# The scan stage of a two-layer kernel: a weight quantised in a turned layout, with its scale rows loaded back from memory

## The chip, the cores and the metric

The kernel runs on one core of a Trainium2 chip. The metric is the device time of one execution in microseconds (us). Before the change the median of three runs is 2079.48 us (2079.25 to 2079.97).

## The reference, cut to what matters

Two layers act on x of shape (2, 4096, 512). In the first, a state-space branch and a quantised linear branch read the same normalised x:

```
x1 = xn @ w1.T + b1;  z = silu(conv(x1));  v = silu(xn @ v1.T + bv1)
h  = h * sigmoid(A) + z_t * B;  y = sum(h * C) + D * z_t      # a scan over 4096 tokens, 512 channels, 16 states
x  = x + (y * v) @ w2.T + b2 + quant(xn) @ quant(Wf).T + bf
```

`quant` takes each row in blocks of 32 elements: scale = max(max|block| / 7.5, 1e-30), the block divided by its scale is rounded to the nearest value of a 6-bit grid, and multiplied by the scale again. For the weight Wf (512 x 512, rows are output features) this gives 16 scales a row. The second layer (linear attention and a gated feed-forward) is not touched.

## The kernel before, in words

The program has four phases, one after the other on each engine's queue: project (x to z and v), scan (z to y), mix (the rest of layer one and the keys of layer two), and the second layer. The change lies in `phase_scan` (L664 to L931).

The scan goes over 64 octets of 8 channels. For octet o, TensorE issues three products of 128x512, each seen as two passes in the trace: `own(o + 1)` (L901, z times the into-table, to the bank that the recurrence reads), the product with the Toeplitz table (L919) and the product of the states with the out-table (L922), which ends y of the octet (semaphore `y_full`). Beside them:

- SyncE loads z (256 KB an octet, L717) six octets ahead, when `y_full` of octet o - 6 is there.
- GpSimd makes the three tables of an octet (L755), three octets ahead at most. TensorE's `own` waits for all three.
- VectorE runs the recurrence (`scan(o + 1)`, L773, two instructions), and behind it in each octet one extra step of the weight's preparation.
- ScalarE takes y out of its bank (`take(o)`, L843) and issues its store to memory (L847). There are four y tiles (`Y = 4`), and `take` of octet o waits until the store of octet o - 4 has landed. TensorE's Toeplitz product of octet o waits for the take of octet o - 2 (`y_done`). ScalarE's queue also issues the weight loads, one 256 KB piece at a time.

The places are octet numbers written out by hand:

```
def take(o):
    act.wait_ge(y_full, o + 1)
    if o >= Y:
        act.wait_ge(y_stored[o % Y], 16 * (o // Y))
```

The feed-forward weight goes this way: ScalarE loads it in its natural layout (output features on partitions) to `wf_nat` at octets 1 to 4 (L860). VectorE quantises it in nine steps at octets 10 to 18 (L792 to L809): a reduce to the block maxima, two steps on 64 scales, a product with the inverse scales, four rounding steps on the 128x2048 tile, a product with the scales. TensorE turns it by 16 transposes at octets 24 to 27 (L908, four banks). ScalarE rounds each bank to the high part (L876), and VectorE subtracts for the low part (L824). At octets 32 to 39 the same split is made for two other weights (ScalarE L852, VectorE L778).

GpSimd has one piece of other work near: at its octet 20, `clear_sums` (three memsets, L1109 and L1111).

Of the kernel before, what the change touches and what calls it, by code (L numbers as in the profile page):

```python
# [3 lines left out]
P = 128  # L4
# [659 lines left out]
def phase_scan(nc, sh, ins, scr, keep, banks, areas, late, mix):  # L664
# [5 lines left out]
    def sem(name):  # L670
        return nc.alloc_semaphore(name)
# [6 lines left out]
    zo += [first_weight.tile(f"c_z{i}", [P, NCH]) for i in range(3, Z)]  # L678
    yo = [first_weight.tile(f"c_y{i}", [P, NCH]) for i in range(Y)]
    q_max = first_weight.tile("c_q_max", [P, KT * D // QBLOCK])  # L680
    q_scale = first_weight.tile("c_q_scale", [P, KT * D // QBLOCK])
    q_inv = first_weight.tile("c_q_inv", [P, KT * D // QBLOCK])
    wf_nat = turned_x.tile("c_wf_nat", [P, KT * D])
    q_work = turned_x.tile("c_q_work", [P, KT * D])
    w2, wf, wk, wv = late["w2"], late["wf"], late["wk"], late["wv"]
    w2_raw, wk_raw = late["w2_raw"], late["wk_raw"]

    z_in = [sem(f"c_z_in{i}") for i in range(Z)]
    y_stored = [sem(f"c_y_stored{i}") for i in range(Y)]
# [5 lines left out]
    wf_in = sem("c_wf_in")  # L695
    w_hi, w_lo = keep["w_hi"], keep["w_lo"]
    HI = 2 * KT
    q_step, f_turned, f_hi = sem("c_q_step"), sem("c_f_turned"), sem("c_f_hi")

    FB, YB, SB = banks[0:4], banks[4:6], banks[6:8]  # L700
    into_t, toep_t, out_pow, mask8 = keep["into_t"], keep["toep_t"], keep["out_pow"], keep["mask8"]
    ident = keep["ident"]
    z_of = scr["z"].rearrange("(o c) r n -> o (c r) n", c=OCTET)
    y_of = scr["y"].rearrange("(o c) m n -> o (c m) n", c=OCTET)
    TURN_AT, WEIGHTS_AT, QUANTISE_AT = 24, 32, 10
    QUANTISED_AT, WEIGHT_PIECES_AT, BIASES_AT = 1, 6, 30
    MIX_IN_AT, MIX_PREPARE_AT, MIX_BANKS_AT, MIX_HEAD_AT = 38, 40, 42, 61
    MIX_TURN_AT = {56: 0, 60: 1}
# [57 lines left out]
    def vector(dve):  # L766
        def scan(o):
            dve.wait_ge(own_full, o + 1)
            if o >= 2:
                dve.wait_ge(y_full, o - 1)  # L770
            rate = keep["decay"][:, o:o + 1].broadcast_to([P, NCB - 1])
            for b in range(B):
                nc.vector.tensor_tensor_scan(state[o % 2][:, b, 1:], rate, SB[o % 2][:, b * NCB:(b + 1) * NCB - 1],  # L773
                                             0.0, ALU.mult, ALU.add).then_inc(state_done, 1)

        def weight_low(i, kt, tile, raw):
            dve.wait_ge(w_hi, HI + KT * i + kt + 1)
            nc.vector.tensor_tensor(tile[:, 1, kt, :], raw[:, kt, :], tile[:, 0, kt, :].bitcast(F32),  # L778
                                    ALU.subtract).then_inc(w_lo, 1)

        blocks = wf_nat[:, :].rearrange("p (b e) -> p b e", e=QBLOCK)
        NB = KT * D // QBLOCK

        def wide(tile):
            return tile[:, :].unsqueeze(2).broadcast_to([P, NB, QBLOCK])

        def quantise_step(k):
            dve.wait_ge(wf_in, 16 * KT)
            if k:
                dve.wait_ge(q_step, k)  # L790
            if k == 0:
                ins_ = nc.vector.tensor_reduce(q_max[:, :], blocks, AX.X, ALU.max, apply_absolute_value=True)  # L792
            elif k == 1:
                ins_ = nc.vector.tensor_scalar(q_scale[:, :], q_max[:, :], 1.0 / FP6_MAX, SCALE_EPS, ALU.mult, ALU.max)
            elif k == 2:
                ins_ = nc.vector.reciprocal(q_inv[:, :], q_scale[:, :])
            elif k == 3:
                ins_ = nc.vector.tensor_tensor(blocks, blocks, wide(q_inv), ALU.mult)
            elif k == 4:
                ins_ = nc.vector.tensor_scalar(q_work[:, :].bitcast(U32), wf_nat[:, :].bitcast(U32), EXPONENT_BITS,  # L800
                                               None, ALU.bitwise_and)
            elif k == 5:
                ins_ = nc.vector.tensor_scalar(q_work[:, :], q_work[:, :], 1.0, ROUND_MAGIC, ALU.max, ALU.mult)
            elif k == 6:
                ins_ = nc.vector.tensor_tensor(wf_nat[:, :], wf_nat[:, :], q_work[:, :], ALU.add)
            elif k == 7:
                ins_ = nc.vector.tensor_tensor(wf_nat[:, :], wf_nat[:, :], q_work[:, :], ALU.subtract)
            else:
                ins_ = nc.vector.tensor_tensor(blocks, blocks, wide(q_scale), ALU.mult)  # L809
            ins_.then_inc(q_step, 1)  # L810

        for i in range(2):
            nc.vector.memset(state[i][:, :, 0:1], 0.0).then_inc(zeroed, 1)
        dve.wait_ge(zeroed, 2)
        scan(0)
        for o in range(NO):
            if o + 1 < NO:
                scan(o + 1)
            if QUANTISE_AT <= o < QUANTISE_AT + 9:
                quantise_step(o - QUANTISE_AT)  # L820
            if TURN_AT <= o - 2 < TURN_AT + KT:
                kt = o - 2 - TURN_AT
                dve.wait_ge(f_hi, kt + 1)
                nc.vector.tensor_tensor(wf[:, 1, kt, :], FB[kt][:, :], wf[:, 0, kt, :].bitcast(F32), ALU.subtract)\  # L824
                  .then_inc(w_lo, 1)
            if WEIGHTS_AT <= o < WEIGHTS_AT + 2 * KT:
                i, kt = divmod(o - WEIGHTS_AT, KT)
                weight_low(i, kt, *((w2, w2_raw), (wk, wk_raw))[i])
            if o == MIX_IN_AT:
                mix["shift"]()  # L830
            if MIX_PREPARE_AT <= o < MIX_PREPARE_AT + 3 * mix["steps"]:
                mix["prepare_step"](*divmod(o - MIX_PREPARE_AT, mix["steps"]))
            if o - 2 in MIX_TURN_AT:
                mix["low_q"](MIX_TURN_AT[o - 2])
            if o == MIX_HEAD_AT:
                mix["gate_front"](0)

    def scalar(act):
# [17 lines left out]
        for o in range(NO):  # L856
            take(o)
            if QUANTISED_AT <= o < QUANTISED_AT + KT:
                t = o - QUANTISED_AT
                act.dma_start(wf_nat[:, t * D:(t + 1) * D], ins["L0_ffn_weight"][t * P:(t + 1) * P, :])\  # L860
                   .then_inc(wf_in, 16)
            if o == WEIGHT_PIECES_AT:
                for h in range(2):
                    act.wait_ge(*project["z"][h])
                    act.wait_ge(*project["v"][h])
                act.wait_ge(*project["powers"])
            if WEIGHT_PIECES_AT <= o < WEIGHT_PIECES_AT + 2 * 3 * KT and (o - WEIGHT_PIECES_AT) % 2 == 0:
                i, kt = divmod((o - WEIGHT_PIECES_AT) // 2, KT)
                tile, name, done = pieces[i]
                act.dma_start(tile[:, kt, :], ins[name][:, kt, :]).then_inc(done, 16)  # L870
            if o in (BIASES_AT, BIASES_AT + 2, BIASES_AT + 4):
                mix["load_bias"]((o - BIASES_AT) // 2)
            if TURN_AT <= o - 1 < TURN_AT + KT:
                kt = o - 1 - TURN_AT
                act.wait_ge(f_turned, kt + 1)
                nc.scalar.activation(wf[:, 0, kt, :], FB[kt][:, :], ACT.Copy).then_inc(f_hi, 1)  # L876
            if WEIGHTS_AT <= o < WEIGHTS_AT + 2 * KT:
                i, kt = divmod(o - WEIGHTS_AT, KT)
                weight_high(i, kt, *((w2, w2_raw), (wk, wk_raw))[i])
# [12 lines left out]
            if o >= NO - 2:  # L892
                mix["set_sums"](o - NO + 3)

    def tensor(pe):
# [5 lines left out]
            pe.matmul(SB[o % 2][:, :], into[o % TABS][:, :, :].rearrange("p c s -> p (c s)"), zo[o % Z][:, :],  # L901
                      start=True, stop=True).then_inc(own_full, 1)

        def turn_weight(kt):
            if kt == 0:
                pe.wait_ge(q_step, 9)
            for ot in range(KT):
                mm = pe.transpose(FB[kt][:, ot * P:(ot + 1) * P], wf_nat[:, ot * D + kt * P:ot * D + (kt + 1) * P],  # L908
                                  ident[:, :])
            mm.then_inc(f_turned, 1)  # L910

        own(0)
        pe.wait_ge(*project["v_taken"])
        for o in range(NO):
            if o + 1 < NO:
                own(o + 1)
            if o >= 2:
# [3 lines left out]
            pe.wait_ge(state_done, B * (o + 1))  # L921
            pe.matmul(YB[o % 2][:, :], outof[o % TABS][:, :, :].rearrange("p c m -> p (c m)"),  # L922
                      state[o % 2][:, :, :].rearrange("p b n -> p (b n)"), start=False, stop=True).then_inc(y_full, 1)
            if TURN_AT <= o < TURN_AT + KT:
                turn_weight(o - TURN_AT)
            if o == MIX_BANKS_AT:
                mix["open_banks"]()
            if o in MIX_TURN_AT:
# [1225 lines left out]
def two_layer_kernel(nc, ins, out):  # L2154
# [3 lines left out]
    def dram(name, shape, dt=F32):  # L2158
# [3 lines left out]
        "x": ins["L0_attn_x"],  # L2162
        "out": out,
        "rows": dram("scr_rows", [sh.NG, 2, sh.GT, P]),
        "kern": dram("scr_kern", [NO, OCTET, 2 * CHUNK]),
        "z": dram("scr_z", [D, CHUNK, sh.NCH]),
        "v": dram("scr_v", [D, CHUNK, sh.NCH]),
# [109 lines left out]
```

## Time and profile before

| | |
|---|---|
| median of three runs | 2079.48 us |
| the profiled execution's own time | 2080.59 us |
| its span, first to last instruction | 2078.8 us |
| TensorE busy | 2063.7 us (99%) |
| VectorE busy | 1523.1 us (73%) |
| ScalarE busy | 1095.0 us (53%) |
| GpSimd busy | 840.9 us (40%) |
| moved by DMA | 263.47 MB |

The profile is of one execution. Times are from the start of the span. DVE is VectorE, ACT ScalarE, POOL GpSimd, PE TensorE's products, PEld its weight loads, SPq and ACTq the DMA issues of SyncE and ScalarE. The scan phase lies between about 369 and 540 us. Time between a DMA's issue and its data's arrival is called landing.

### The profile page before, as it was taken

What the parts mean: (1) busy time and instruction counts of PE and PEld (TensorE: products, weight loads), DVE (VectorE), ACT (ScalarE), POOL (GpSimd) and SP (SyncE); (2) the same over time, 40 slices, a digit from 0 to 9 for tenths busy, and PEclk for the clock granted to TensorE, in tenths of its full rate; (3) what the DMA queues carried; (4) which work ended last, traced back from release to release, by engine and by line L of the source; (5) the groups of instructions that cost most, each with busy time, mean ns of one, the idle gap of its engine ahead of it and who ended that gap; (6) DMA issues with size and microseconds to landing.
All of it is one profiled execution on the core that took longest, in us unless ns stands there. A gap on an engine that the chain in (4) does not pass through costs nothing.

```text
span 2078.8 us, 27463 instructions
## 1 busy us (share of the span) xinstructions
PE 2063.7 (99%) x9263; PEld 1645.9 (79%) x9263; DVE 1523.1 (73%) x2973; ACT 1095.0 (53%) x1842; POOL 840.9 (40%) x842
## 2 busy tenths in 40 slices
PE   9999999999999999999999999999999999999998
PEld 7887888444688888888888888788888888888887
DVE  6998775666787777776777875677777676677776
ACT  4555556223455555555555555755555555555553
POOL 1011110455545454554444453144444444444444
PEclk9999999999999999999999999999999999999999
DMA  5666662976533333333333332422222222222211
GB/s 199 251 220 226 202 210 103 292 254 208 176 122 102 108 116 103 131 102 102 122 119 105 115 119 101 152 71 72 71 72 74 90 91 86 88 71 72 71 41 41
DMA packets 179750, 263.47 MB, mean 127 GB/s; under 512 B 20377, under 2 KB 110745, under 8 KB 177050
## 3 DMA queue, kind: packets, MB, share of 16 engines
q1 hardware_dynamic: 166488, 238.18, 34.7%
q10 hardware_dynamic: 13122, 23.53, 3.1%
q8 instruction: 74, 1.21, 0.3%
q14 instruction: 66, 0.54, 0.1%
HBM read 160.88 MB, written 100.79 MB: 126 GB/s over the span
## 4 chain that ended last, share of the span: by engine, by line
PE 89%; DVE 5%; ACT 2%; issue 2%; POOL 1%; DMA 1%; SPq 0%; POOLq 0%; ACTq 0%
PE bank L102 23%; PE bank L104 23%; PE bank L103 23%; PE bank L1512 7%; PE bank L2068 3%; PE bank L901 3%; PE bank L922 3%; PE bank L919 3%; PE bank L1468 2%; PE bank L645 1%; DVE e_w_lo L1895 0%; DVE d_x L1364 0%; DVE d_xq L1335 0%; DVE d_stats L1366 0%; PE bank L1526 0%
## 5 line engine op out<-in xcount | busy, mean ns | idle before, releaser
L102 PE MATMUL bank<-e_ring,e_w_hi 128*128 128x512 f32 x512 | 200.8, 392 | 0.0
L103 PE MATMUL bank<-e_ring,e_w_hi 128*128 128x512 f32 x512 | 199.3, 389 | 0.0
L104 PE MATMUL bank<-e_ring,e_w_lo 128*128 128x512 f32 x512 | 199.3, 389 | 0.0
L1512 PE MATMUL bank<-d_kh,d_nat 128*128 128x512 f32 x768 | 191.1, 398 | 0.0
L1788 POOL TENSOR_TENSOR e_x<-e_x,e_beta 128x512 f32<-128x512 f32 x64 | 91.5, 1449 | 220.7 <-ACT e_y L1831 220.7
L1133 POOL TENSOR_TENSOR rstd<-d_var_eps,neg_half 128x1 f32<-128x1 f32 x64 | 35.7, 558 | 340.7 <-DVE d_var_eps L1375 340.7
L1842 ACT ACTIVATE e_kr<-bank 128x512 f32<-128x512 f32 x64 | 38.0, 594 | 247.6 <-PE bank L104 247.6
L1512 PEld LDWEIGHTS bank<-d_kh,d_nat 128*128 128x128 f32 x768 | 139.7, 188 | 26.9
L1913 DVE TENSOR_TENSOR e_ring<-e_mixed,e_ring 128x512 fp32r<-128x512 f32 x128 | 93.5, 731 | 88.0 <-ACT e_ring L1806 87.9
L1770 POOL TENSOR_TENSOR e_x<-e_x,e_ff 128x512 f32<-128x512 f32 x64 | 83.4, 1304 | 174.9 <-DVE e_ff L1979 174.9
L1380 DVE TENSOR_TENSOR d_nat<-d_xn,d_nat 128x512 fp32r<-128x512 f32 x64 | 86.0, 1345 | 78.1 <-ACT d_nat L1240 78.1
L1904 DVE SCALAR_TENSOR_TENSOR e_mixed<-e_xt,cols,e_prev 128x512 f32<-128x512 f32 x128 | 104.0, 813 | 41.3 <-ACT e_prev L1817 40.8
L1222 ACT ACTIVATE d_xt<-bank 128x512 f32<-128x512 f32 x64 | 38.3, 598 | 166.7 <-PE bank L1468 166.6
L773 DVE TENSOR_TENSOR_SCAN c_state<-decay,bank 128x255 f32<-128x255 f32 x128 | 80.4, 670 | 53.2 <-PE bank L901 53.1
L311 POOL TENSOR_TENSOR b_rstd<-b_var_eps,neg_half 128x4 f32<-128x4 f32 x16 | 16.2, 1011 | 247.2 <-DVE b_var_eps L367 247.2
L102 PEld LDWEIGHTS bank<-e_ring,e_w_hi 128*128 128x128 f32 x512 | 96.1, 188 | 20.4 <-issue 0.9
L1806 ACT ACTIVATE e_ring<-e_mixed 128x512 fp32r<-128x512 f32 x128 | 80.8, 632 | 59.7 <-DVE e_mixed L1904 57.4
L1774 POOL TENSOR_TENSOR e_y<-e_y,e_att 128x512 f32<-128x512 f32 x64 | 107.1, 1673 | 12.7 <-DVE e_att L1998 12.7
L104 PEld LDWEIGHTS bank<-e_ring,e_w_lo 128*128 128x128 f32 x512 | 96.1, 188 | 20.1
L103 PEld LDWEIGHTS bank<-e_ring,e_w_hi 128*128 128x128 f32 x512 | 96.1, 188 | 19.3
L102 PE MATMUL bank<-e_w_hi,e_keys 128*128 128x512 f32 x256 | 103.7, 405 | 0.2 <-DVE e_ff L1979 0.2
L102 PE MATMUL bank<-d_w,d_ut 128*128 128x512 f32 x256 | 100.2, 391 | 2.1 <-POOL d_ut L1121 2.1
(226 smaller groups left out, 6300.0 us busy)
## 6 DMA issues: line engine op xcount, KB each, us to landing
scr_v<-b_vt SPq DMA_DIRECT2D x64, 256.0 KB, 2.7
scr_z<-b_zt SPq DMA_DIRECT2D x64, 256.0 KB, 2.1
c_z<-scr_z SPq DMA_DIRECT2D x64, 256.0 KB, 4.3
scr_y<-c_y ACTq DMA_DIRECT2D x64, 256.0 KB, 4.0
d_x<-in_L_attn_x SPq DMA_DIRECT2D x64, 256.0 KB, 3.6
d_v<-scr_v SPq DMA_DIRECT2D x32, 512.0 KB, 5.2
scr_x<-d_x SPq DMA_DIRECT2D x64, 256.0 KB, 2.3
scr_xnt<-d_xt SPq DMA_DIRECT2D x32, 512.0 KB, 4.1
```

The costliest lines, as they stand in the source:

```text
L102: eng.matmul(out, lhs[hi], rhs[hi], start=first, stop=False, skip_group_check=onto)
L103: eng.matmul(out, lhs[hi], rhs[lo], start=False, stop=False, skip_group_check=onto)
L104: return eng.matmul(out, lhs[lo], rhs[hi], start=False, stop=last, skip_group_check=onto)
L773: nc.vector.tensor_tensor_scan(state[o % 2][:, b, 1:], rate, SB[o % 2][:, b * NCB:(b + 1) * NCB - 1], 0.0, ALU.mult, ALU.add).then_inc(sta ...
L1380: nc.vector.tensor_tensor(nat[q][:, 1, :], xn[N % 2][:, :], nat[q][:, 0, :].bitcast(F32), ALU.subtract).then_inc(nat_lo, 1)
L1512: mm = pe.matmul(BG[c][:, :], s[:, i, cols], r[:, j, :], start=M % NTB == 0 and i == j, stop=M % NTB == NTB - 1 and i == 1, skip_group_che ...
L1770: nc.gpsimd.tensor_tensor(x2[h][:, t, :], x2[h][:, t, :], ff[t % 2][:, :], ALU.add).then_inc(base_done, 1)
L1774: nc.gpsimd.tensor_tensor(y[t][:, :], y[t][:, :], att[t % 2][:, :], ALU.add).then_inc(sum_done, 1)
L1788: nc.gpsimd.tensor_tensor(x2[h][:, t, :], x2[h][:, t, :], beta[:, :], ALU.add).then_inc(shifted, 1)
L1806: nc.scalar.activation(ring[slot][:, 0, kt, :], src, ACT.Copy).then_inc(hi_done, 1)
L1904: nc.vector.scalar_tensor_tensor(mixed[kt % 2][:, :], current(g % 2, kt), mu[:, kt:kt + 1], prev[kt % 2][:, :], ALU.mult, ALU.add).then_in ...
L1913: nc.vector.tensor_tensor(ring[slot][:, 1, kt, :], src, ring[slot][:, 0, kt, :].bitcast(F32), ALU.subtract).then_inc(lo_done, 1)
```

## The change

The weight also comes from the host in the turned layout (`ffn_turned`, input features on partitions), and the quantisation works on that layout in `wf_raw`, which is the place of the low part of `wf`. The block maxima are still found on the natural layout, at octet 6. Scales and inverse scales are computed at octets 7 and 8 into 32 columns for each of the four groups of 128 rows, and turned by four VectorE transposes of 32x32 blocks at octet 9. At octet 10 ScalarE's queue stores them in four DMAs to a 32x512 array in memory. At octet 13 it loads from there two tiles of 128x2048 (the inverse scales to `q_work`, the scales to `wf_nat`), 1 MB each: partition group s of 32 reads the same row of 2048 numbers. Six VectorE steps at octets 24 to 29 then quantise the turned weight. The 16 transposes on TensorE go. The turned weight's four pieces of 256 KB are loaded at octets 7, 9, 11 and 13 on ScalarE's queue. The high parts are rounded at octets 30 to 33 and the low parts at 31 to 34.

```
@@ phase_scan: tiles, semaphores, banks, octets @@
-    q_scale = first_weight.tile("c_q_scale", [P, KT * D // QBLOCK])
-    q_inv = first_weight.tile("c_q_inv", [P, KT * D // QBLOCK])
+    q_cols = first_weight.tile("c_q_cols", [P, KT, QBLOCK])
+    q_turned = first_weight.tile("c_q_turned", [P, KT, QBLOCK])
...
-    q_step, f_turned, f_hi = sem("c_q_step"), sem("c_f_turned"), sem("c_f_hi")
-    FB, YB, SB = banks[0:4], banks[4:6], banks[6:8]
+    q_step, f_hi = sem("c_q_step"), sem("c_f_hi")
+    wf_raw_in = sem("c_wf_raw_in")
+    YB, SB = banks[4:6], banks[6:8]
...
-    TURN_AT, WEIGHTS_AT, QUANTISE_AT = 24, 32, 10
+    ROUNDED_AT, WEIGHTS_AT, SCALES_AT, SCALES_OUT_AT, ROWS_IN_AT, QUANTISE_AT = 29, 32, 6, 10, 13, 24
+    SCALE_STEPS, QUANTISE_STEPS = 3 + KT, 6
@@ VectorE @@
+        def scale_step(k):
+            if k:
+                dve.wait_ge(q_step, min(k, 3))
+            scales = q_cols[:, :, KT * KT:2 * KT * KT]
+            if k == 0:
+                dve.wait_ge(wf_in, 16 * KT)
+                ins_ = nc.vector.tensor_reduce(q_max[:, :], wf_nat[:, :].rearrange("p (b e) -> p b e", e=QBLOCK), AX.X,
+                                               ALU.max, apply_absolute_value=True)
+            elif k == 1:
+                for t in range(KT):
+                    ins_ = nc.vector.tensor_scalar(scales[:, t, :].rearrange("p (s k) -> p k s", k=KT),
+                                                   q_max[:, t * KT * KT:(t + 1) * KT * KT]
+                                                   .rearrange("p (k s) -> p k s", k=KT),
+                                                   1.0 / FP6_MAX, SCALE_EPS, ALU.mult, ALU.max)
+            elif k == 2:
+                ins_ = nc.vector.reciprocal(q_cols[:, :, 0:KT * KT], scales)
+            else:
+                ins_ = nc.vector.transpose(q_turned[:, k - 3, :], q_cols[:, k - 3, :])
+            ins_.then_inc(q_step, 1)
+
         def quantise_step(k):
-            dve.wait_ge(wf_in, 16 * KT)
-            if k:
-                dve.wait_ge(q_step, k)
+            dve.wait_ge(q_step, SCALE_STEPS + k)
+            wf_turned = wf_raw[:, :, :].rearrange("p k d -> p (k d)")
             if k == 0:
-                ins_ = nc.vector.tensor_reduce(q_max[:, :], blocks, AX.X, ALU.max, apply_absolute_value=True)
...
-            elif k == 3:
-                ins_ = nc.vector.tensor_tensor(blocks, blocks, wide(q_inv), ALU.mult)
+                dve.wait_ge(wf_in, 16 * (2 * KT + 2))
+                dve.wait_ge(wf_raw_in, 16 * KT)
+                ins_ = nc.vector.tensor_tensor(wf_turned, wf_turned, q_work[:, :], ALU.mult)
...
             else:
-                ins_ = nc.vector.tensor_tensor(blocks, blocks, wide(q_scale), ALU.mult)
+                ins_ = nc.vector.tensor_tensor(wf_turned, wf_turned, wf_nat[:, :], ALU.mult)
@@ VectorE, the loop over octets @@
-            if QUANTISE_AT <= o < QUANTISE_AT + 9:
+            if SCALES_AT <= o < SCALES_AT + 3:
+                scale_step(o - SCALES_AT)
+            if o == SCALES_AT + 3:
+                for k in range(3, SCALE_STEPS):
+                    scale_step(k)
+            if QUANTISE_AT <= o < QUANTISE_AT + QUANTISE_STEPS:
                 quantise_step(o - QUANTISE_AT)
-            if TURN_AT <= o - 2 < TURN_AT + KT:
-                kt = o - 2 - TURN_AT
+            if ROUNDED_AT <= o - 2 < ROUNDED_AT + KT:
+                kt = o - 2 - ROUNDED_AT
                 dve.wait_ge(f_hi, kt + 1)
-                nc.vector.tensor_tensor(wf[:, 1, kt, :], FB[kt][:, :], wf[:, 0, kt, :].bitcast(F32), ALU.subtract)\
+                nc.vector.tensor_tensor(wf[:, 1, kt, :], wf_raw[:, kt, :], wf[:, 0, kt, :].bitcast(F32), ALU.subtract)\
@@ ScalarE, the loop over octets @@
+            if o == SCALES_OUT_AT:
+                act.wait_ge(q_step, SCALE_STEPS)
+                for s in range(P // QBLOCK):
+                    act.dma_start(scr["f_scales"].rearrange("c (t s i) -> s c t i", t=KT, s=P // QBLOCK)[s],
+                                  q_turned[s * QBLOCK:(s + 1) * QBLOCK, :, :]).then_inc(wf_in, 16)
+            if o == ROWS_IN_AT:
+                act.wait_ge(wf_in, 16 * 2 * KT)
+                for w, tile in enumerate((q_work, wf_nat)):
+                    rows = bass.AP(scr["f_scales"].tensor, w * KT * KT * D,
+                                   [[KT * D, P // QBLOCK], [0, QBLOCK], [1, KT * D]])
+                    act.dma_start(tile[:, :], rows).then_inc(wf_in, 16)
...
+            if WEIGHT_PIECES_AT <= o < WEIGHT_PIECES_AT + 2 * KT and (o - WEIGHT_PIECES_AT) % 2:
+                kt = (o - WEIGHT_PIECES_AT) // 2
+                act.dma_start(wf_raw[:, kt, :], ins["ffn_turned"][:, kt, :]).then_inc(wf_raw_in, 16)
...
-            if TURN_AT <= o - 1 < TURN_AT + KT:
-                kt = o - 1 - TURN_AT
-                act.wait_ge(f_turned, kt + 1)
-                nc.scalar.activation(wf[:, 0, kt, :], FB[kt][:, :], ACT.Copy).then_inc(f_hi, 1)
+            if ROUNDED_AT <= o - 1 < ROUNDED_AT + KT:
+                kt = o - 1 - ROUNDED_AT
+                act.wait_ge(q_step, SCALE_STEPS + QUANTISE_STEPS)
+                nc.scalar.activation(wf[:, 0, kt, :], wf_raw[:, kt, :], ACT.Copy).then_inc(f_hi, 1)
@@ TensorE @@
-        def turn_weight(kt):
-            if kt == 0:
-                pe.wait_ge(q_step, 9)
-            for ot in range(KT):
-                mm = pe.transpose(FB[kt][:, ot * P:(ot + 1) * P], wf_nat[:, ot * D + kt * P:ot * D + (kt + 1) * P],
-                                  ident[:, :])
-            mm.then_inc(f_turned, 1)
...
-            if TURN_AT <= o < TURN_AT + KT:
-                turn_weight(o - TURN_AT)
@@ two_layer_kernel, kernel @@
+        "f_scales": dram("scr_f_scales", [QBLOCK, D]),
...
+    laid["ffn_turned"] = raw["L0_ffn_weight"].T.reshape(KT, P, 512).transpose(1, 0, 2)
```

## Rows read from the trace of the kernel before

**Rows 1.** The page: busy time by engine, and the chain that ended last by line.
```profile
PE 2063.7 (99%) x9263; PEld 1645.9 (79%) x9263; DVE 1523.1 (73%) x2973; ACT 1095.0 (53%) x1842; POOL 840.9 (40%) x842
PE bank L102 23%; PE bank L104 23%; PE bank L103 23%; PE bank L1512 7%; PE bank L2068 3%; PE bank L901 3%; PE bank L922 3%; PE bank L919 3%; PE bank L1468 2%; PE bank L645 1%; DVE e_w_lo L1895 0%; DVE d_x L1364 0%; DVE d_xq L1335 0%; DVE d_stats L1366 0%; PE bank L1526 0%
```

**Rows 2.** The chain of waits in the scan: start us, us, what.
```profile
378.36 0.86 PE bank L901 x2
...
406.68 0.86 PE bank L901 x2
...
427.42 0.86 PE bank L901 x2
...
435.15 0.86 PE bank L901 x2
...
447.20 0.86 PE bank L901 x2
```

**Rows 3.** Timeline, 406 to 425 us: start, us, engine, line, op [idle before].
```profile
406.18 2.27 DVE L798 TENSOR_TENSOR c_wf_nat<-c_wf_nat,c_q_inv 128x2048 f32<-128x2048 f32 x1
406.77 1.95 POOL L755 TENSOR_TENSOR c_into<-into_t,consts 128x128 f32<-128x128 f32 x1 [1.45 <-PE bank L922]
...
409.03 0.40 POOL L755 TENSOR_TENSOR c_outof<-out_pow,consts 128x128 f32<-128x128 f32 x1
...
409.53 1.10 PE L901 MATMUL bank<-c_z,c_into 128*128 128x512 f32 x2 [0.28 <-issue]
...
420.78 0.98 POOL L1111 MEMSET d_kacc<- 128x512 f32 x2
...
421.27 2.26 DVE L809 TENSOR_TENSOR c_wf_nat<-c_wf_nat,c_q_scale 128x2048 f32<-128x2048 f32 x1
...
421.72 2.07 POOL L755 TENSOR_TENSOR c_into<-into_t,consts 128x128 f32<-128x128 f32 x1
...
424.61 1.10 PE L901 MATMUL bank<-c_z,c_into 128*128 128x512 f32 x2 [0.90 <-issue]
```

**Rows 4.** Timeline of two undisturbed ScalarE takes and of one scan.
```profile
373.25 0.60 ACT L843 ACTIVATE c_y<-bank 128x512 f32<-128x512 f32 x1 [4.04 <-PE bank L922]
...
389.56 1.26 DVE L773 TENSOR_TENSOR_SCAN c_state<-decay,bank 128x255 f32<-128x255 f32 x2 [1.31 <-PE bank L901]
...
406.72 0.60 ACT L843 ACTIVATE c_y<-bank 128x512 f32<-128x512 f32 x1 [1.98 <-PE bank L922]
```

**Rows 5.** Timeline: weight piece, reduce and small steps; then octet 32.
```profile
383.55 0.35 ACTq L860 DMA_DIRECT2D c_wf_nat<-in_L_ffn_weight  x1
...
398.46 2.26 DVE L792 TENSOR_REDUCE c_q_max<-c_wf_nat 128x64 f32<-128x2048 f32 x1
...
399.04 0.40 POOL L755 TENSOR_TENSOR c_into<-into_t,consts 128x128 f32<-128x128 f32 x1 [1.45 <-PE bank L922]
...
401.80 0.27 DVE L794 TENSOR_SCALAR c_q_scale<-c_q_max 128x64 f32<-128x64 f32 x1
...
460.61 0.62 ACT L852 ACTIVATE d_w<-d_w_raw 128x512 fp32r<-128x512 f32 x1
...
461.27 0.69 DVE L778 TENSOR_TENSOR d_w<-d_w_raw,d_w 128x512 fp32r<-128x512 f32 x1 [1.60 <-ACT d_w L852]
```

**Rows 6.** DMA issues of the whole run: names, queue, count, KB, us to landing.
```profile
c_z<-scr_z SPq DMA_DIRECT2D x64, 256.0 KB, 4.3
scr_y<-c_y ACTq DMA_DIRECT2D x64, 256.0 KB, 4.0
b_xc<-in_x_turned SPq DMA_DIRECT2D x14, 1024.0 KB, 7.1
b_rows<-scr_rows SPq DMA_DIRECT2D x14, 512.0 KB, 5.4
```

**Rows 7.** Windows: stretch, busy by engine (count), clock, DMA share, GB/s.
```profile
16.00:18.00 2.00, 2.00 (x11) 1.62 (x10) 2.00 (x4) 2.00 (x5) 0.00 (x0) 1.00 1.06 427
...
370.00:380.00 10.00, 10.00 (x25) 4.37 (x24) 5.67 (x10) 1.79 (x3) 4.29 (x10) 1.00 1.05 358
```

More of the change, by code:

```diff
@@ L685, in phase_scan @@
     w2, wf, wk, wv = late["w2"], late["wf"], late["wk"], late["wv"]
-    w2_raw, wk_raw = late["w2_raw"], late["wk_raw"]
+    w2_raw, wf_raw, wk_raw = late["w2_raw"], late["wf_raw"], late["wk_raw"]
     z_in = [sem(f"c_z_in{i}") for i in range(Z)]
@@ L697, in phase_scan @@
     HI = 2 * KT
-    q_step, f_turned, f_hi = sem("c_q_step"), sem("c_f_turned"), sem("c_f_hi")
-    FB, YB, SB = banks[0:4], banks[4:6], banks[6:8]
+    q_step, f_hi = sem("c_q_step"), sem("c_f_hi")
+    wf_raw_in = sem("c_wf_raw_in")
+    YB, SB = banks[4:6], banks[6:8]
     into_t, toep_t, out_pow, mask8 = keep["into_t"], keep["toep_t"], keep["out_pow"], keep["mask8"]
-    ident = keep["ident"]
     z_of = scr["z"].rearrange("(o c) r n -> o (c r) n", c=OCTET)
     y_of = scr["y"].rearrange("(o c) m n -> o (c m) n", c=OCTET)
-    TURN_AT, WEIGHTS_AT, QUANTISE_AT = 24, 32, 10
+    ROUNDED_AT, WEIGHTS_AT, SCALES_AT, SCALES_OUT_AT, ROWS_IN_AT, QUANTISE_AT = 29, 32, 6, 10, 13, 24
+    SCALE_STEPS, QUANTISE_STEPS = 3 + KT, 6
     QUANTISED_AT, WEIGHT_PIECES_AT, BIASES_AT = 1, 6, 30
@@ L779, in weight_low @@
                                     ALU.subtract).then_inc(w_lo, 1)
[L781 to L785, printed above, removed]
+        def scale_step(k):
[17 more added lines that the diff above has]
+            ins_.then_inc(q_step, 1)
@@ L793, in quantise_step @@
             elif k == 1:
-                ins_ = nc.vector.tensor_scalar(q_scale[:, :], q_max[:, :], 1.0 / FP6_MAX, SCALE_EPS, ALU.mult, ALU.max)
+                ins_ = nc.vector.tensor_scalar(q_work[:, :].bitcast(U32), wf_turned.bitcast(U32), EXPONENT_BITS,
+                                               None, ALU.bitwise_and)
             elif k == 2:
-                ins_ = nc.vector.reciprocal(q_inv[:, :], q_scale[:, :])
+                ins_ = nc.vector.tensor_scalar(q_work[:, :], q_work[:, :], 1.0, ROUND_MAGIC, ALU.max, ALU.mult)
@@ L797, in quantise_step @@
             elif k == 3:
-                ins_ = nc.vector.tensor_tensor(blocks, blocks, wide(q_inv), ALU.mult)
+                ins_ = nc.vector.tensor_tensor(wf_turned, wf_turned, q_work[:, :], ALU.add)
             elif k == 4:
[L800 to L807, printed above, removed]
+                ins_ = nc.vector.tensor_tensor(wf_turned, wf_turned, q_work[:, :], ALU.subtract)
```

## The prediction

> **What bounds the kernel now.** I read the page first. TensorE is busy for 2063.7 us of 2078.8 and the chain that ended last runs over its products almost alone [rows 1], so an edit counts by what it takes from TensorE's queue or makes that queue wait. Next the chain in the scan. An undisturbed octet is 2.575 us: its first product starts at 378.36 and, 11 octets on, at 406.68 [rows 2]. Six passes of 0.43 us fill that time, so there TensorE is the bound. The chain shows two disturbed stretches. From 406.68 to 427.42 seven octets take 20.74 us where 18.02 are due: 2.72 us lost. From 435.15 to 447.20 four octets take 12.05 for 10.30: 1.75 us, the 16 transposes [rows 2].
>
> The timeline explains the first stretch. A two-input VectorE step on the 128x2048 tile runs from 406.18 to 408.45. GpSimd's table product beside it takes 1.95 us, and ends 0.27 us after that step [rows 3]; beside the reduce at 398.46 the same table product takes 0.40 [rows 5]. The tables of that octet are complete at 409.43, and TensorE, 0.28 us idle, starts at 409.53 [rows 3]. So the loss is GpSimd held up by the rounding steps, not the recurrence being late. The worst gap, 0.90 us at 424.61, has one more cause: the memsets of `clear_sums` (0.98 us from 420.78) pushed the table product into the last step, which began at 421.27 [rows 3].
>
> **What goes.** The 16 transposes: -1.75 us, all on TensorE's queue, with nothing in their place.
>
> **What moves.** Six large VectorE steps of the same kinds and sizes (2.27 and 2.26 us for those shown in [rows 3], the other four likewise the same operations on the same shape) go from octets 13 to 18 to octets 24 to 29. GpSimd makes tables there too, so their 2.72 us come again, less the part of the memsets, which stay at octet 20 in an idle stretch of GpSimd. Without them the first table of that octet would be done before 421.27, and one table product of 0.40 us less would be queued behind the step: -0.4 us (bounds: 0 and -1.0, all of the memset). Both inputs of the two products with the scales are now full tiles; before, one was read as a broadcast. 2.27 and 2.26 us for those against about the same for the others leaves nothing to price.
>
> **What VectorE does new at octets 6 to 9.** The reduce (2.26 us [rows 5]) needs the fourth weight piece, issued at 383.55; transfers of that size on this queue land in 4.0 us at the median [rows 6]; taking 5.3 to be careful gives 388.9. It then ends at 391.1, and the recurrence due at 389.56 [rows 4] starts 1.5 us late. TensorE needs its result four product pairs later: own at 388.5, needed at 388.5 + 2.575 + 2 x 0.86 = 392.8, and the recurrence takes 1.26 [rows 4], so it may start up to about 391.4. Hidden, with 0.3 to spare (bounds 0 and +0.3). Four scale steps on 16 columns and the inverse: 0.27 us for 64 columns [rows 5] gives at most 1.1 and 0.5, hidden in the 1.31 us that VectorE idles each octet [rows 4]. The four VectorE transposes are not in the trace; from below a 64-column step each (0.27), from above a 512-column subtract each (0.69 [rows 5]), so 1.1 to 2.8 us together; I take 1.1, hidden, at the other end about +0.1.
>
> **Octets 31 to 34.** The low parts now share octets 32 to 34 with those of the next weight. Today the ScalarE rounding is done 461.23 and VectorE waits 1.60 us for it [rows 5]. A second rounding in front adds 0.62 us. The recurrence behind is then some 1.5 us late instead of 0.9, at the edge of what is free: +0.1 us (0 to +0.4).
>
> **What the queue gets.** This decides. The take of octet 0 is at 373.25 and that of octet 13 at 406.72 [rows 4]. There ScalarE issues, in this order, the two row loads (2 x 1,048,576 bytes), the last turned-weight piece and then the store of y of octet 13. Its own waits are covered: the four small stores were issued at octet 10, 7.7 us earlier, and loads and stores here land in 4 to 5. The take of octet 17, due 10.3 us later at 417.0, waits until that store has landed, and on each DMA engine the store's bytes come behind the rows' bytes of the same queue. Behind the take waits the Toeplitz product of octet 19, due at 407.54 + 5 x 2.575 = 420.4, and with it everything on TensorE.
>
> How long the row loads hold the queue depends on how many of the 16 DMA engines share them, and no row shows a load of this form: the nearest have 128 partitions' rows outermost on both sides, the 1 MB load of 8 KB rows (7.1 us) and the 512 KB load in which every partition reads the same row (5.4 us) [rows 6]. The new source pattern has 4 outermost (four groups, then 32 repeats, then 8 KB). So from below it is spread like the nearest rows, over 16 engines; from above over 4, one for each group. A transfer has to be cut along a dimension that both sides have, the outer one, and 4 is all that this source offers: I take 4. That departs from the nearest rows on purpose, since they lack just this.
>
> An engine's rate: 358 GB/s in a stretch where the engines are full and loads and stores mix, 427 where only loads run [rows 7], a sixteenth of each is 22.4 and 26.7 GB/s; I take 24.5. On each of the four engines lie 524,288 bytes of rows, 16,384 of the weight piece and 16,384 of the store, and beside them six z loads (SyncE gets to issue those for y of octets 13 to 18) of 16,384 each: 655,360 bytes, 26.7 us. From 407.2 with 1.0 us for the arrival (a 256 KB store lands in 4.0 though its bytes need 0.7; I allow less since the queue is already running) that is 434.9. The take ends at 435.6, and TensorE has waited 435.6 - 420.4 = 15.2 us (29.3 us at the slow rate give 17.8, 24.5 at the fast one 13.0). The stores of octets 14 to 16 lie directly behind, 0.7 to 1.4 us apart, against 2.6 us an octet: no further wait. Z was loaded ahead meanwhile. The rows have landed before octet 24.
>
> The clock: it is granted in full in every stretch read, and the longest gap in those of the scan is 0.90 us [rows 3, 7]. A gap of 15 us may let it fall to the lower level, 1.2 GHz. One octet at half speed costs 2.6 us; bounds 0 and 2.6, I take 1.3.
>
> The Trainium skill, "DMA: Bandwidth & Descriptors", in its section on why a DMA increments its semaphore by 16, says that a transfer is divided along the slowest dimension over the largest number of engines up to 16 that divides both sides' counts; its table of recommendations warns of just such a small outermost dimension. By that rule the row loads run on 4 engines and the sum is the one below; by the nearest rows, taken as they are, it is that of the first rival. No row of this trace tests it.
>
> **Sum.** -1.75 - 0.4 + 0.1 + 15.2 + 1.3 = +14.5 us. The profiled execution took 2080.59 us (span 2078.8), so 2095.1; the median of the runs shown lies 1.1 us below it, which gives 2094.0.
>
> **Rivals.**
> 1. *The row loads spread over all 16 engines (not slower).* An engine has 131,072 + 32,768 + three z loads of 16,384 = 212,992 bytes, 8.7 us; the store lands at 416.9, before the take asks at 417.0, and 2.8 us of TensorE's lead lie behind that. What is left is -1.75 - 0.4 + 0.1: 2077.4. For it: the two nearest rows. Against: their outer 128. The wait decides from about 11 engines down: the take may start until 419.8, so 11.6 us, 284 KB an engine, of which some 100 are other traffic. With 8 engines it is 14.7 us and a wait of 3 us, about 2080. Chance 0.21, with 0.03 for something between.
> 2. *Four engines, and slow ones.* One engine reads the same 8 KB 32 times, beside z loads of 2 KB pieces. At half the rate the 26.7 us become 53 and the wait 42: 2121. For it: nothing in the trace; against: the 512 KB load that repeats one row for all partitions lands in 5.4 us [rows 6]. Chance 0.06.
> 3. The forecast: 0.70. Its own range, by rate and clock: 2089 to 2100.
>
> **How the numbers follow.** Leaving out only the slow case and the far edges, the range goes from just under rival 1 to above the forecast's upper end: 2076.5 to 2102. A difference counts from 0.2%, 4.2 us, which is about what a measurement of this kernel can tell from no change. Rival 1 is 2.1 us faster, so within; the forecast and rival 2 are slower: slower 0.76, same 0.22, faster 0.02.
>
> **What would show it.** The landing of the two c_q_work and c_wf_nat loads from scr_f_scales: above 20 us for the forecast, under 10 for rival 1. The landing of the y store at 408: some 27 us. One TensorE gap of 13 to 18 us before L919 near 420, and ScalarE's c_y waiting for the store (DMA scr_y) instead of for TensorE. A DMA share near 0.4 to 0.5 in that gap, not 1.0. Near octets 24 to 29 gaps in front of L901 of about 2.3 us in all, with table products of about 2 us on GpSimd; no matmul on consts and c_wf_nat. It is wrong if the store of octet 13 lands within 11 us; the step at fault is then the count of engines.

## The result, and the profile after

| | before | after |
|---|---|---|
| median of four timed runs | 2079.36 us (2079.25 to 2079.97) | 2101.86 us (2099.13 to 2104.87) |
| profiled execution, own time | 2080.59 us | 2100.61 us |
| its span, granted clock | 2078.8 us, 0.999 | 2098.8 us, 0.995 |

The ratio is 1.0106, with the interval 1.0095 to 1.0118: slower by 22.5 us in the medians. Between the two profiled executions it is 20.0 us: the scan takes 21.5 us more (from the take of octet 0 to that of the last octet, 371.66 to 560.69 against 373.25 to 540.77), and it begins 1.6 us earlier, behind code that the change doesn't touch. The first rows are the page of after; they answer to [rows 1].

```profile
PE 2066.9 (98%) x9247; PEld 1645.6 (78%) x9247; DVE 1522.4 (73%) x2980; ACT 1094.8 (52%) x1842; POOL 840.4 (40%) x842
PE bank L102 22%; PE bank L104 22%; PE bank L103 22%; PE bank L1533 7%; PE bank L2089 3%; PE bank L942 2%; PE bank L932 2%; PE bank L945 2%; PE bank L1489 2%; DMA scr_y<-c_y 2%; DVE e_w_lo L1916 0%; DVE d_x L1385 0%; DVE d_xq L1356 0%; DVE d_stats L1387 0%; PE bank L1547 0%
```

A DMA is now among what the chain runs over: `DMA scr_y<-c_y`, 2% of the span. TensorE has 16 instructions fewer and 3.2 us more busy time; its mean granted clock is 0.995 for 0.999, so some of its products ran slower. The chain of waits in order of time (start us, us, what) shows where, and answers to [rows 2]; in this kernel L932 is the product into the state, L942 the Toeplitz product, L945 the one out of the state, L860 ScalarE's take.

```profile
403.53 0.86 PE bank L942 x2
...
405.29 0.60 ACT c_y L860
...
407.12 31.55 DMA scr_y<-c_y
...
438.75 0.61 ACT c_y L860
...
439.40 2.08 PE bank L942 x2
441.48 1.71 PE bank L945 x2
443.19 1.71 PE bank L932 x2
...
447.83 0.86 PE bank L942 x2
```

From 403.53 to 447.83 eight octets take 44.30 us where 8 x 2.575 = 20.60 are due: 23.7 lost. The store of y of octet 13, issued at 407.12, lands after 31.55 us; in the run before, such a store lands in 4.0 at the median [rows 6]. ScalarE's and TensorE's timelines of that stretch:

```profile
407.12 3.49 ACTq L864 DMA_DIRECT2D scr_y<-c_y  x1
410.71 0.60 ACT L860 ACTIVATE c_y<-bank 128x512 f32<-128x512 f32 x1 [4.82 <-PE bank L945]
410.72 3.29 ACTq L898 DMA_DIRECT2D d_wk_raw<-in_L_attn_Wk  x1
414.05 5.90 ACTq L864 DMA_DIRECT2D scr_y<-c_y  x1
420.06 0.60 ACT L860 ACTIVATE c_y<-bank 128x512 f32<-128x512 f32 x1 [8.75 <-issue]
...
438.75 0.60 ACT L860 ACTIVATE c_y<-bank 128x512 f32<-128x512 f32 x1 [15.47 <-DMA scr_y<-c_y]
```

```profile
420.70 2.07 PE L942 MATMUL bank<-c_z,c_toep 128*128 128x512 f32 x2 [6.51 <-ACT c_y L860]
422.57 1.92 PE L945 MATMUL bank<-c_state,c_outof 128*128 128x512 f32 x2
...
425.50 1.02 PE L942 MATMUL bank<-c_z,c_toep 128*128 128x512 f32 x2
...
439.40 2.08 PE L942 MATMUL bank<-c_z,c_toep 128*128 128x512 f32 x2 [11.16 <-ACT c_y L860]
```

There are two gaps. Before the second, ScalarE waits 15.47 us for the landing of the store: the gap of the forecast. Before the first it waits for no semaphore at all. It is still issuing: the three DMA instructions from 407.12 on last 3.49, 3.29 and 5.90 us, where such an issue mostly takes 0.33 to 0.36 elsewhere, and the take of octet 15 sits behind them. Read with the windows of the same stretch, which answer to [rows 7]:

```profile
412.00:416.00 4.00, 2.20 (x6) 0.65 (x4) 1.81 (x3) 0.00 (x0) 1.12 (x3) 1.00 0.71 225
416.00:420.00 4.00, 0.00 (x0) 0.00 (x0) 0.00 (x0) 0.00 (x0) 0.00 (x0) 0.77 0.32 108
420.00:424.00 4.00, 3.29 (x4) 1.51 (x5) 0.00 (x0) 1.19 (x2) 0.00 (x0) 0.50 0.52 203
...
432.00:436.00 4.00, 0.00 (x0) 0.00 (x0) 0.00 (x0) 0.00 (x0) 0.00 (x0) 0.50 0.25 102
```

The last three numbers of a row are the granted clock, the DMA share and GB/s. In the last row no engine has any work, and the DMA share is a quarter: 4 of 16 engines, at 102 / 4 = 25.5 GB/s each. The z loads that SyncE issues between 404 and 440 us, on its own queue, land after 6.1 to 11.9 us; before the change they take 2.9 to 5.4. They are late, but far less than the store. The granted clock falls to 0.50 within each gap, and the products behind it run at 1.2 GHz (2.07 us for what takes 1.02 at 425.50).

The steps that the forecast hid are hidden. The timeline of VectorE at octets 6 to 9 answers to [rows 5]:

```profile
387.42 2.29 DVE L789 TENSOR_REDUCE c_q_max<-c_wf_nat 128x64 f32<-128x2048 f32 x1 [0.61 <-DMA c_wf_nat<-in_L_ffn_weight]
...
390.79 0.49 DVE L793 TENSOR_SCALAR c_q_cols<-c_q_max 128x16 f32<-128x16 f32 x4
...
392.35 0.52 DVE L798 RECIPROCAL c_q_cols<-c_q_cols 128x64 f32<-128x64 f32 x1
...
394.44 0.47 DVE L800 STREAM_TRANSPOSE c_q_turned<-c_q_cols 128x32 f32<-128x32 f32 x4
```

The chain knows no gap there. In the quantise stretch (octets 24 to 29) it does:

```profile
454.69 0.86 PE bank L932 x2
...
459.84 0.27 issue
460.11 1.10 PE bank L932 x2
...
474.29 0.32 issue
474.61 1.10 PE bank L932 x2
...
477.42 0.86 PE bank L932 x2
```

Four such gaps (0.27, 0.28, 0.31, 0.32), each followed by a product pair of 1.10 for 0.86; eight octets take 22.73 for 20.60, so 2.13 us, against 2.72 before. From 477.42 to 502 the chain has no gap at all.

### The profile page after: what moved, and what is told of

The parts are those of the page before. It is cut to its first block, busy times and chain, and to the rows that moved or that the text cites. A ratio compares the mean times of both kernels' runs of the same rounds, so it can differ in the third digit from the quotient of the medians.

```text
span 2098.8 us, 27441 instructions
## 1 busy us (share of the span) xinstructions
PE 2066.9 (98%) x9247; PEld 1645.6 (78%) x9247; DVE 1522.4 (73%) x2980; ACT 1094.8 (52%) x1842; POOL 840.4 (40%) x842
## 4 chain that ended last, share of the span: by engine, by line
PE 87%; DVE 5%; DMA 2%; ACT 2%; issue 2%; POOL 1%; SPq 0%; ACTq 0%; POOLq 0%
PE bank L102 22%; PE bank L104 22%; PE bank L103 22%; PE bank L1533 7%; PE bank L2089 3%; PE bank L942 2%; PE bank L932 2%; PE bank L945 2%; PE bank L1489 2%; DMA scr_y<-c_y 2%; DVE e_w_lo L1916 0%; DVE d_x L1385 0%; DVE d_xq L1356 0%; DVE d_stats L1387 0%; PE bank L1547 0%
## 5 line engine op out<-in xcount | busy, mean ns | idle before, releaser
L860 ACT ACTIVATE c_y<-bank 128x512 f32<-128x512 f32 x64 | 38.2, 596 | 139.1 <-PE bank L945 108.9
```

## The experiments

All ran beside the kernel before, whose medians in these comparisons are 2079.75 to 2080.16 us. The theory under test: the source pattern `[[KT * D, 4], [0, 32], [1, KT * D]]` puts both loads on 4 of 16 DMA engines, and all that passes through these four is late. Rivals: the repeated reading of one row is slow, or the order in the queue alone does it.

**e1_split: sixteen engines by smaller loads.** The same bytes in the same octet and queue; each load is cut in four, of 32 partitions, whose outer dimension is now the partition.

```
-                    rows = bass.AP(..., w * KT * KT * D, [[KT * D, P // QBLOCK], [0, QBLOCK], [1, KT * D]])
-                    act.dma_start(tile[:, :], rows).then_inc(wf_in, 16)
+                    for s in range(P // QBLOCK):
+                        rows = bass.AP(..., (w * KT + s) * KT * D, [[0, QBLOCK], [1, KT * D]])
+                        act.dma_start(tile[s * QBLOCK:(s + 1) * QBLOCK, :], rows).then_inc(wf_in, 16)
```

> The changed kernel with each 1 MB row load cut into four loads of 256 KB, one for each group of 32 partitions, at the same octet on the same queue: same bytes, same memory rows read 32 times, but the outermost count is 32 in place of 4. Theory (the row loads ran on 4 of the 16 DMA engines, and the y store of octet 13 queued behind them): TensorE's two waits near 414 and 428 us go, the DMA share near octet 13 is close to 1 for some 7 us in place of 0.25, the store lands in under 12 us, and what is left of the change is its gain: 2079.4 - 1.75 (transposes) - 0.6 (the quantise stretch as measured after) = 2077.0, within 2076 to 2079. Rival A (reading the same 8 KB row for 32 partitions is slow in itself) and rival B (2 MB more is too much for this stretch): about 2095 to 2105 as in the changed kernel.

2085.72 us (2084.62 to 2086.92, 7 runs), ratio 1.0029 [1.0017, 1.0040]. It is 16 us faster than after, and no window shows a quarter any more, so the number of engines is most of the cost. But 2077 is missed by 8.7. The chain holds one store of y:

```profile
410.93 14.56 DMA scr_y<-c_y
```

and the windows show why it needs 14.56 us:

```profile
412.00:416.00 4.00, 4.00 (x10) 1.82 (x10) 2.25 (x4) 1.26 (x3) 1.72 (x5) 1.00 1.01 229
416.00:420.00 4.00, 3.26 (x8) 1.14 (x6) 1.53 (x3) 0.00 (x0) 2.74 (x8) 1.00 1.02 241
...
424.00:428.00 4.00, 1.78 (x2) 0.84 (x3) 0.00 (x0) 1.06 (x2) 0.00 (x0) 0.50 1.05 405
```

All 16 engines are busy, and they move 229 to 241 GB/s; as soon as the rows are in, 405. So a second cost was uncovered: a load into 32 partitions occupies 16 engines at little over half their rate. TensorE waits 5.1 us for it and 0.7 for a z load, and the three product pairs behind take 2.5 us more than at the full clock: 8.3 of the 8.7. The Trainium skill, "SBUF — State Buffer", section "Door 1: The DMA port swizzle", says that partitions 0 to 31 (and 0 to 63) reach only 8 of the 16 ports on SBUF's DMA side, and measures 189 GB/s for 1 MiB into 32 partitions against 328 into 128. The trace agrees in size: 229 against 405, in mixed traffic. That the ports are the reason, no run here shows.

**f1_distinct and f2_allparts: reading or writing?** The first is e1 with 32 different source rows for each load (the scales are left out: it reads `x_turned`). The second is after's two 1 MB loads with the one row repeated for all 128 partitions, outermost (the same scales everywhere).

```
+                        rows = bass.AP(ins["x_turned"].tensor, (w * KT + s) * QBLOCK * KT * D, [[KT * D, QBLOCK], [1, KT * D]])
```

```
+                                   [[0, P], [1, KT * D]])
```

> The split form of the row loads (eight loads to 32 partitions each) with its source changed to 32 distinct 8 KB rows of the input for each load; the weight's scales are then not the right ones, all else is the same work. In the split form the DMA engines were busy (share 1.0) at only 209 to 250 GB/s from 410 to 422 us, and the y store of octet 13 took 14.6 us. Theory P (the writing side: 32 partitions at a time take no more than that): no change, store 13 to 16 us, GB/s 200 to 260 at share 1, 2085.5 (2083.5 to 2087.5). Theory R (the reading side: one memory row read by all engines at once is slow): GB/s rises to 350 or more, the store lands in under 11 us, and the time falls to 2077 to 2079.

> The changed kernel with each 1 MB load reading one and the same 8 KB row for all 128 partitions (outermost count 128), so two whole-tile loads and the wrong scales. Theory P (writing side): all partitions are reached at once, engines busy at 350 GB/s or more for some 7 us, y store of octet 13 in 8 to 11 us, 2077 to 2079. Theory R (reading side): the same row is read even more often, so 209 to 250 GB/s at share 1 again and 2084 or more. Both leave the four-engine theory alone: the share must not go to 0.25.

f1: 2085.66 us (2084.08 to 2086.74), ratio 1.0025, the same as e1, and its store of octet 13 lands after 15.09 us; where the rows are read plays no part. f2: 2078.09 us (2077.50 to 2078.83), ratio 0.9990 [0.9980, 1.0001]. Its windows, with one row read 128 times:

```profile
408.00:412.00 4.00, 4.00 (x11) 1.84 (x10) 2.05 (x4) 0.97 (x2) 2.07 (x6) 1.00 1.03 415
...
416.00:420.00 4.00, 3.21 (x8) 1.25 (x7) 2.33 (x4) 0.60 (x1) 2.74 (x8) 1.00 1.03 392
```

So 2 MB at that place and from one row are nearly free when they are spread over 16 engines and 128 partitions. Nearly: its store of octet 13 lands after 12.26 us (8 to 11 were expected) and TensorE waits 0.8. The first rival of the prediction described this kernel (2077.4), and it lay at the edge of its slack.

f2 differs from e1 in two things, 128 partitions for 32 and two loads for eight. The number of loads doesn't explain the rate: the transfers of 256 KB that follow the rows in e1, over 128 partitions each, run at 405 GB/s. It does add issuing time. Issuing eight row loads and the weight piece keeps ScalarE for 4.6 us before the store in e1, issuing two and the piece for 1.5 in f2; from the first row load's issue to the landing of the store it is 19.2 us in e1 and 13.8 in f2. How much of these 5.4 us is issuing isn't separated.

**e2_half: only one of the two loads split.** c_q_work stays in the narrow form, c_wf_nat is cut in four.

> The changed kernel with only the load of the scales cut into four, that of the inverse scales left in the form with 4 outermost. Theory: each of the four engines has 262,144 + 65,536 + 32,768 + five z loads of 16,384 = 442,368 bytes, at 25.5 GB/s 17.3 us; the store of octet 13 lands some 18 us after the row loads' issue, TensorE waits about 6 us once and loses 2 to 3 us to the clock: 2085.5 (2081 to 2090). The DMA share shows a stretch near 0.25 of under 10 us. Rivals A and B (same reads and bytes): 2095 to 2105.

2101.20 us (2101.18 to 2101.22), ratio 1.010: as slow as after. The expectation (2085.5) is missed. It counted half the narrow bytes as half the wait. The windows:

```profile
412.00:416.00 4.00, 4.00 (x11) 1.78 (x10) 2.52 (x4) 0.60 (x1) 1.51 (x5) 1.00 1.00 209
...
432.00:436.00 4.00, 0.00 (x0) 0.00 (x0) 0.00 (x0) 0.00 (x0) 0.00 (x0) 0.50 0.25 72
```

At first all 16 engines are busy at 209 GB/s; afterwards four of them are still at work alone, at 72 to 86 GB/s. The store of octet 13 lands after 30.83 us, and the issue of that of octet 16 lasts 9.11. The two costs seem to add up rather than replace one another; no run separates them further.

**e3_sync and e4_pool: another queue for the narrow loads.** e3 issues them from SyncE ahead of the z load of octet 19, e4 from GpSimd; ScalarE's queue is free of them.

```
+            if o - Z == ROWS_IN_AT:
+                sp.wait_ge(wf_in, 16 * 2 * KT)
...
+                    sp.dma_start(tile[:, :], rows).then_inc(wf_in, 16)
```

> The changed kernel with both row loads, in the form with 4 outermost, issued on SyncE's queue ahead of the z load of octet 19. Theory (what waits is what stands behind in the same queue): y stores land in under 10 us and ScalarE is not held; the z load of octet 19 lands after some 27 us and TensorE waits for it before the first product of octet 19, one gap of about 17 us, plus 3 us for the clock: 2097 (2091 to 2101). Rival C (the four engines are simply full for everybody, whatever the queue): y stores land late too and ScalarE waits for them as in the changed kernel.

> The changed kernel with both row loads, in the form with 4 outermost, on GpSimd's own queue, so that neither z loads nor y stores stand behind them. Theory (waiting in one queue): the engines share between queues, y stores and z loads land in under 12 us, and there is no long wait: 2077 to 2081, the upper end if GpSimd's issuing holds up one octet's tables. Rival C: y stores or z loads land after 20 us or more and the time stays above 2090.

e3: 2106.53 us (2105.70 to 2107.36), ratio 1.013, slower than after and above the expected range. ScalarE's issues are short again (0.33 to 0.36 us), and now SyncE's are long: its z issues from 406 us on last 0.49 to 4.64 us, where they take 0.32 in after. So the long issues go with the queue that the narrow loads are in. The z loads stand behind the rows now; the chain:

```profile
406.31 36.02 DMA c_z<-scr_z
```

and TensorE waits once, 27.0 us:

```profile
PE bank L932 <- DMA c_z<-scr_z: 27.0, 1, 27.0
```

The other half of the expectation is missed: the y stores should have landed in under 10 us, and those issued from 405 to 419 us take 12.5 to 24.9, though they stand in a queue without rows; ScalarE waits 4.9 us for one. So rival C holds in part: a transfer in the same queue is hit hardest, one in the other queue too.

e4: 2098.43 us (2098.16 to 2098.70), ratio 1.009; expected were 2077 to 2081, the largest miss of the series. The expectation took a queue of its own for enough, since each engine would then serve y and z in turn with the rows. Over 400 to 440 us (names, queue, count, KB, median us to landing):

```profile
c_z<-scr_z SPq DMA_DIRECT2D x9, 256.0 KB, 17.7
scr_y<-c_y ACTq DMA_DIRECT2D x9, 256.0 KB, 13.8
...
c_wf_nat<-scr_f_scales POOLq DMA_DIRECT2D x1, 1024.0 KB, 39.9
```

Every queue is late. The DMA share tells another story than in after, though:

```profile
426.00:428.00 2.00, 1.31 (x2) 0.80 (x3) 0.00 (x0) 0.00 (x0) 0.00 (x0) 0.50 0.53 102
```

In windows of 2 us it stays near 1 until 424 us and doesn't fall below 0.49 up to 436; it is never a quarter. That the rows lie on the same four engines here is therefore not shown, and neither is why a share of 0.53 moves only 102 GB/s. If each engine served the queues in turn, piece by piece, the rows' pieces of 8 KB would crowd out pieces of 2 KB; no run varied the size of a piece, so the cause stays open. What is shown: the narrow loads make y and z late from each of the three queues.

**g1_spread: the split loads, one every second octet.** Octets 13 to 27, each 256 KB; the step that needs q_work waits for its four, the last step for c_wf_nat.

```
+            if ROWS_IN_AT <= o < ROWS_IN_AT + 4 * KT and (o - ROWS_IN_AT) % 2 == 0:
+                w, s = divmod((o - ROWS_IN_AT) // 2, KT)
```

> The split form with one of the eight loads an octet, at every second octet from 13 to 27 (those of the scales are needed only by the last quantise step, at octet 29). Theory: 51 GB/s more for 16 octets beside 204 of z and y and 51 of weight pieces, nothing piles up before a y store, no wait of TensorE for a y tile: 2079.6 - 1.75 - 0.6 = 2077.2 (2076.2 to 2078.2). If the extra 2 MB cost by themselves wherever they are put: 2080 or more.

2077.63 us (2076.47 to 2080.85, 10 runs), ratio 0.9991 [0.9982, 1.0000]. The first five windows from 404 us on show 289 to 373 GB/s at the full clock, and no gap of TensorE but those of the quantise steps. With the whole DMA cost gone, the rest of the change is worth 2.4 us in the medians, as the terms of the sum said (-1.75 - 0.4); the interval just reaches 1.

**b1_noturn and b2_halves: the two remaining terms by themselves**, on the kernel before. b1 leaves the 16 transposes out (the weight goes on unturned, read from `wf_nat` where before it was read from the banks). b2 cuts the four two-input steps of the rounding in two, 128x1024 each, over octets 10 to 22; all else as before.

```
-            if TURN_AT <= o < TURN_AT + KT:
-                turn_weight(o - TURN_AT)
```

```
+            k, half = [(0, None), (1, None), (2, None), (3, 0), (3, 1), (4, None), (5, None), (6, 0), (6, 1), (7, 0), (7, 1),
+                       (8, 0), (8, 1)][k]
```

> The kernel before, with the 16 transposes of the feed-forward weight left out of TensorE's queue in octets 24 to 27 and nothing else of the change; its high and low parts are made from wf_nat as it lies, so the weight goes on unturned (left out: the turning). Theory (the transposes' 1.75 us in the chain of before are all on the path): 1.75 below before, 2077.6 against 2079.4, and the chain of octets 24 to 27 takes 10.30 us for its four octets instead of 12.05. Rival (something else in those octets, the recurrence or the tables, is as late as the transposes are long, so that taking them out only turns them into a wait): under 0.5 us gained, 2079.0 to 2079.5, with TensorE idle in that stretch.

> The kernel before, with its four two-input VectorE steps on the 128x2048 tile (the product with the inverse scales, the sum, the difference, the product with the scales) each cut into two of 128x1024, one an octet: 13 steps at octets 10 to 22 instead of 9 at 10 to 18; weight layout, transposes and loads as before. Theory (GpSimd's table product is held for as long as a two-input VectorE step lasts; a hold of 1.2 us leaves it on time, one of 2.27 does not): the 2.72 us lost before L919 in that stretch go, 2076.7 to 2077.0. Rival (the gain of the halves in the split form came from the scales' own layout, full tiles in place of a broadcast): 0 to 0.5 us gained, 2079.

b1: 2078.31 us (2077.48 to 2079.21, 11 runs) against 2080.16, ratio 0.9992 [0.9983, 1.0000]: -1.85 for -1.75 expected, at the edge of what the runs resolve, so the chain has to carry it. Its chain runs through octets 24 to 27 at 0.86 a pair, with nothing late in their place. b2: 2077.43 us (2076.98 to 2078.49, 11 runs), ratio 0.9987 [0.9978, 0.9996]: -2.73 for -2.72. Its timeline:

```profile
404.91 1.20 DVE L802 TENSOR_TENSOR c_wf_nat<-c_wf_nat,c_q_inv 128x1024 f32<-128x1024 f32 x1
...
405.50 0.88 POOL L755 TENSOR_TENSOR c_into<-into_t,consts 128x128 f32<-128x128 f32 x1 [1.46 <-PE bank L926]
```

A half step takes 1.20 us, and the table product beside it 0.88 instead of 1.95 [rows 3]; it still ends behind the step, but the tables are in time. The only rows of b2's chain from 395 to 478 us that aren't a product pair at 0.86 are the last product of a pair at 394.69 and the four groups of transposes, such as

```profile
433.74 0.44 PE bank L912 x4
```

**g2_halves: both together**, the spread split loads (octets 13 to 17, 19, 21, 23) and the halved two-input steps (10 steps at octets 20 to 29).

```
+    PIECES_AT = [13, 14, 15, 16, 17, 19, 21, 23]
...
+            which, half = [(0, 0), (0, 1), (1, None), (2, None), (3, 0), (3, 1), (4, 0), (4, 1), (5, 0), (5, 1)][k]
```

> As the spread form, and the four two-input quantise steps each cut into two halves of 1024 columns in two octets (ten steps at octets 20 to 29, the loads at 13, 14, 15, 16, 17, 19, 21, 23). Theory (GpSimd's tables are held up by as long as one two-input step lasts, and 1.28 us of that is free): at 1.13 us a step the tables come in time and the 2.1 us that the quantise stretch still lost go too: 2075.1 (2074.2 to 2076.5). Rival (the loss is VectorE's total work, or the recurrence late behind it): 2077 as the spread form. Its own risk: five loads in five octets, which would show as ScalarE waiting for scr_y.

2075.19 us (2074.53 to 2075.87, 9 runs), ratio 0.9975 [0.9965, 0.9985]: 4.8 us faster than the kernel before, and 26.7 than after. Its chain from 375 to 477 us consists of product pairs at 0.86 us alone. The two terms measured alone, 1.85 + 2.73 = 4.58, add up to it.

## Why the prediction was right, and where its sizes were off

**The mechanism and the sign: right.** Four engines, by the quarter of the DMA share at 432; the store of octet 13 held, by the chain; the take of octet 17 behind it, by ScalarE's timeline. e1 and f2 take the four engines away, and 16 and 24 us go with them. The rule of the Trainium skill that the prediction cited, "DMA: Bandwidth & Descriptors", on why a DMA increments its semaphore by 16 (divided along the slowest dimension), agrees with this trace: a share of 0.25. Not all signs came out as named. The DMA share in the long gap is 0.25, not 0.4 to 0.5; there are two gaps, not one; and the first sign, the landings of the two row loads, can't be read, since the trace of after has no landing time for them.

**The wait: the term of the sum that was mis-sized, 20.4 us for 15.2.** Without any wait the product that stands behind the take of octet 17 is due six octets after 403.53, at 403.53 + 15.45 = 418.98; it starts at 439.40. Of the 5.2 us too few, 1.4 lie ahead of the store: the scan ran 1.4 us earlier here (take of octet 13 at 405.29, for 406.72), but the store was issued when the forecast had it, at 407.12, since the issues of the two row loads and of the weight piece took 0.60, 0.56 and 0.55 us in front of it, and the forecast had left them out. The other 3.8 are the landing: 31.55 us for 27.7. The rate was about right: 25.5 GB/s an engine from 432 to 436 us, for 24.5 taken. If it held over all of the 31.55 us, that would be 804 KB on an engine where 655 were counted (an estimate); what the rest was isn't settled, the weight pieces and stores behind it in the queue are candidates.

**The first gap: not forecast, and free.** The prediction had the stores of octets 14 to 16 "directly behind" that of octet 13 and gave their issues no time. In after ScalarE is held in three issues of 3.3 to 5.9 us, and with it the take and TensorE (6.51 us, and 2.2 of slow products behind). But by the chain the end of the second gap is set by the store of octet 13 alone, and that was already on its way: what the first gap took was lead that the second wait would have used up anyway. That is read from the chain; no run takes the first gap away by itself. e3 shows that the holding goes with the queue. Busy engines alone don't cause it: in e1, at a share of 1.0, ScalarE's issues last 0.33 to 0.71 us. What does is open.

**The clock: 3.3 us for 1.3, beyond its bound of 2.6.** After the second gap the octet from 439.40 to 444.89 takes 5.49 us, 2.9 over, and the next pair 1.22 for 0.86. The clock comes back after a little more than an octet; the bound had assumed one. With 20.4 this gives the 23.7 of the chain.

**Removed and moved work.** The transposes: -1.75 in the chain, -1.85 by b1. The quantise stretch: -0.59 for -0.4, within its bounds. Octets 31 to 34: nothing for 0.1. The scale steps hidden, the four VectorE transposes 0.47 us together, below the lower bound of 1.1. The sum by what was measured: 20.4 + 3.3 - 1.75 - 0.59 = +21.4, for +21.5 us of the scan; the forecast had +14.5. 2101.86 lies just inside the range (2102.0), and that is luck: both large terms came out above their upper bounds (20.4 for 17.8 at most, 3.3 for 2.6), the forecast's own range of 2089 to 2100 was missed, and two of the four runs lie above 2102.

**The rivals.** The first (16 engines) is no story of this kernel, but f2 is that kernel, and took 2078.09 for 2077.4. The second (four slow engines, 53 us) falls: an engine moves 25.5 GB/s, and f1 and f2 show that reading one row again and again costs nothing.

## What to carry to other kernels

Look at the outermost dimension of both sides of every DMA before you price it: here a leading group count of 4 made two loads of 1 MB hold four engines for some 30 us. What stood behind them in the same queue landed after 31.55 us (36.02 in e3), what passed in the other queue after 6.1 to 11.9 (12.5 to 24.9 in e3). Splitting by 32 partitions brings back the engines but not the rate. Spreading the split loads in time cost nothing measurable. A pattern with 128 partitions outermost was nearly free too, but f2 has the wrong scales: the right ones would need a source laid out for it, which no run tried. And if VectorE's two-input steps hold GpSimd up, cut them in two: here that gave 2.73 us, against 1.85 for all the 16 transposes taken off TensorE.

## What the runs showed of the hardware that was not expected

- Behind the narrow loads a DMA instruction on ScalarE's queue lasted 3.3 to 5.9 us in after, and up to 9.11 in e2; ScalarE ran nothing else meanwhile. With the loads on SyncE's queue it was 0.33 to 0.36, and SyncE's own took up to 4.64.
- Eight loads of 256 KB into 32 partitions each: a DMA share of 1.0 at 229 to 241 GB/s (e1); two of 1 MB into 128 partitions: 364 to 415 GB/s (f2).
- A queue of its own did not shield y and z from the rows: median landings of 13.8 and 17.7 us in e4, with up to 29 for z and 32 for y, where 4.0 and 4.3 are usual [rows 6].
- The clock stood at 0.50 by the end of a gap of 6.5 us already, and that gap cost 2.2 us more in slow products: a third of its length again.
